# Weights staged through twelve slots and compared while they are copied; x, residual loads and y stores begun by GpSimd

## The reference

```
xn = layernorm(x)                                        # x: 16 x 512 x 512, float32
q, k, v = split(xn @ w_qkv.T + b_qkv)                    # 16 heads of 32
p = softmax(q @ k.T / sqrt(32) + causal)                 # per head 512 x 512
att = (p @ v) @ w_out.T + b_out
g = (xn @ gate.T) * gate_s;  u = (xn @ up.T) * up_s      # 1408 inner features, weights -1, 0, 1
ffn = ((silu(g) * u) @ down.T) * down_s
out = x + att + ffn
```

## Time and profile before

| | |
|---|---|
| Median of 3 runs | 2051.01 us (2050.69 to 2054.36) |
| Profiled execution, its own time | 2044.33 us |
| Its span, first to last instruction | 2041.0 us |
| Mean granted TensorE clock | 0.98 of full speed |
| Busy: PE, DVE, ACT, POOL | 1891.5, 1695.2, 1330.5, 1007.2 us |
| DMA: begun by SP's queue | 307.39 MB, 73.4% of 16 engines' span |

### The profile page before, as it was taken

How to read it: one execution, slowest core, us unless ns; L and a number is a source line. 1 busy time by engine, 2 the same in 40 slices (tenths; PEclk the granted TensorE clock), 3 DMA queues, 4 the chain that set the end, 5 groups by cost and what they waited for, 6 DMA issues and landing times.

```text
span 2041.0 us, 43778 instructions
## 1 busy us (share of the span) xinstructions
PE 1891.5 (93%) x14978; PEld 1225.1 (60%) x14978; DVE 1695.2 (83%) x5066; ACT 1330.5 (65%) x3723; POOL 1007.2 (49%) x1389
## 2 busy tenths in 40 slices
PE   5679999999999999999999999999999999989986
PEld 3447566665666656566665666656566665756663
DVE  3668888888888888888888898888888788888885
ACT  3747676665766667666666766666666666767673
POOL 5554554554554454554544545454554555454342
PEclk8889999999999999999999999999999999999998
DMA  6866867778677776868869787777877768676674
GB/s 196 222 125 128 185 133 163 153 136 177 134 165 146 149 162 136 179 133 163 153 135 181 139 163 150 145 175 129 180 136 161 142 137 175 130 171 122 132 147 94
DMA packets 832981, 310.24 MB, mean 152 GB/s; under 512 B 756464, under 2 KB 789232, under 8 KB 832752
## 3 DMA queue, kind: packets, MB, share of 16 engines
q1 hardware_dynamic: 832752, 307.39, 73.4%
HBM read 55.59 MB, written 16.78 MB: 35 GB/s over the span
## 4 chain that ended last, share of the span: by engine, by line
PE 39%; DVE 28%; SPq 14%; DMA 8%; ACT 6%; issue 4%; POOL 0%; DVEq 0%; ACTq 0%; POOLq 0%
PE bank L245 39%; SPq L819 10%; DVE phl L525 8%; DMA pt<-phl 7%; DVE bank L515 5%; ACT phl L428 4%; DVE fh L537 3%; DVE ft L533 2%; DVE small L506 2%; ACT bank L436 2%; DVE res L549 1%; SPq L826 1%; DVE small L487 1%; DVE xhl L660 1%; SPq L812 1%
## 5 line engine op out<-in xcount | busy, mean ns | idle before, releaser
L428 ACT ACTIVATE phl<-bank,small 128x512 f16<-128x512 f32 (+3 forms) x1024 | 500.2, 531 | 322.4 <-DVE small L506 217.7
L436 ACT ACTIVATE bank<-bank,small 128x512 f32<-128x512 f32 (+3 forms) x1024 | 514.4, 503 | 225.5 <-DVE small L515 218.6
L525 DVE SCALAR_TENSOR_TENSOR phl<-bank,small,phl 128x512 f16<-128x512 f32 (+3 forms) x1024 | 525.3, 544 | 102.1 <-ACT phl L428 98.3
L515 DVE CUSTOM_DVE_ANT_0 bank<-bank,mask 128x512 f32<-128x512 f32 (+3 forms) x1024 | 486.0, 505 | 109.3 <-PE bank L245 109.1
L718 POOL TENSOR_SCALAR ht<-fh 128x256 f16<-128x256 f32 x352 | 142.2, 404 | 602.1 <-DVE fh L537 602.1
L245 PE MATMUL bank<-xnT,wg 128*128 128x256 f16 x2816 | 368.0, 274 | 15.8 <-POOL wu L687 6.0
L245 PE MATMUL bank<-xnT,wu 128*128 128x256 f16 x2816 | 368.4, 274 | 0.0
L245 PE MATMUL bank<-xnT,wqkv 128*128 128x512 f16 x1536 | 355.9, 382 | 11.1 <-DMA xnT<-xhl 8.1
L245 PE MATMUL bank<-wd,ht 128*128 128x512 f16 x1408 | 330.4, 392 | 0.0
L245 PEld LDWEIGHTS bank<-xnT,wg 128*128 128x128 f16 x2816 | 262.2, 98 | 82.6 <-issue 13.2
L245 PEld LDWEIGHTS bank<-xnT,wu 128*128 128x128 f16 x2816 | 277.1, 98 | 33.5
(11 more groups left out here) (95 smaller groups left out, 1911.8 us busy)
## 6 DMA issues: line engine op xcount, KB each, us to landing
stk<-qkp SPq DMA_DIRECT2D x768, 64.0 KB, 2.1
res<-in_x_dram SPq DMA_DIRECT2D x64, 256.0 KB, 3.1
out_dram<-res SPq DMA_DIRECT2D x64, 256.0 KB, 2.4
xin<-in_x_dram SPq DMA_DIRECT2D x60, 256.0 KB, 3.2
pt<-phl SPq DMA_TRANSPOSE x512, 3.7
xin<-in_gate_dram SPq DMA_DIRECT2D x11, 256.0 KB, 3.3
xin<-in_up_dram SPq DMA_DIRECT2D x11, 256.0 KB, 3.3
xin<-in_down_dram SPq DMA_DIRECT2D x11, 256.0 KB, 3.4
```

The source lines that it names most:

```text
L428: i = eng.activation(phl[qt][:, j % 2, 0], pb[:, off:off + W], ACT.Copy, scale=st_r[:, c:c + 1])
L436: i = eng.activation(pb[:, off:off + W], pb[:, off:off + W], ACT.Exp, bias=st_m[:, c:c + 1], scale=-1.0, accum_out=st_s[:, c:c + 1])
L515: i = eng.tensor_tensor_reduce(out=bk[:, off:off + W], in0=bk[:, off:off + W], in1=mask[:, 512 - W:512], scale=-(32.0 ** -0.5) / (QS * QS) ...
L525: i = eng.scalar_tensor_tensor(phl[qt][:, j % 2, 1], pb[:, off:off + W], st_r[:, c:c + 1], phl[qt][:, j % 2, 0], ALU.mult, ALU.subtract)
```

## The change

Seven things change together.

- **Twelve staging slots**: four in the `res` tiles, four in `att`, four in `xnT[1]`. The first 24 chunks go through all twelve, the later ones through the first eight. The first 20 chunks are converted ahead of unit 0, then two per unit until unit 14; SP loads them two units ahead instead of three.
- **GpSimd converts all 33 plain chunks**, with a clamp to -1 and 1 in place of two multiplications by one. ScalarE converts none of them.
- **The check follows at once**: VectorE compares the staged float32 chunk with its 16-bit copy, one unit after the conversion (12 chunks ahead of unit 0, 21 in units 1 to 13), and a slot is free when that is done. The second loads and the reductions for the largest magnitude are gone; the clamp takes their place.
- **GpSimd begins the x loads, the residual loads and the y stores** (of the last batch SP still stores y), each with the wait that SP had.
- **Residual loads one unit later**: 12, 13, 15, 17 of the batch instead of 11, 12, 14, 16; the bias addition four units behind follows.
- **Layer norm of batch 1** at units 0, 4, 8, 12 like the others.
- **The stacking of q and k** goes by pairs of heads, with a semaphore each, so that the first five units of a group wait for the first pair only.

```diff
-            norm_at[12 + 2 * t if b == 1 else 40 * b - 40 + 4 * t] = (b, t)
-    check_at = {}
-    per = -(-3 * NI // (B - 5))
-    for i in range(3 * NI):
-        b, r = divmod(i, per)
-        check_at[40 * (b + 2) - 18 + 6 * r] = i
-    xin_order = sorted([(n, "norm", v) for n, v in norm_at.items()] + [(n, "check", v) for n, v in check_at.items()])
-    xin_use = {(kind, v): i for i, (n, kind, v) in enumerate(xin_order)}
-    xin_load_at = {n - 4: i for i, (n, kind, v) in enumerate(xin_order)}
-    nxs = {v: 4 + i for i, v in enumerate(v for n, kind, v in xin_order if kind == "norm")}
+            norm_at[40 * b - 40 + 4 * t] = (b, t)
+    xin_load_at = {n - 4: v for n, v in norm_at.items()}
     res_at = {}
     for b in range(B):
         for t in range(4):
-            res_at[15 + t if b == 0 else 40 * b + (11, 12, 14, 16)[t]] = (b, t)
+            res_at[15 + t if b == 0 else 40 * b + (12, 13, 15, 17)[t]] = (b, t)
...
-    stage = [xnT[1][:, 2 * i:2 * i + 2, :].rearrange("p a b -> p (a b)").bitcast(F32) for i in range(4)]
-    stage += [res[i][:, :] for i in range(4)]
+
+    stage = [res[i][:, :] for i in range(4)]
+    stage += [att[:, i // 2, 2 * (i % 2):2 * (i % 2) + 2, :].rearrange("p a b -> p (a b)").bitcast(F32) for i in range(4)]
+    stage += [xnT[1][:, 2 * i:2 * i + 2, :].rearrange("p a b -> p (a b)").bitcast(F32) for i in range(4)]
...
-        chunks.append(("plain", ("wg", i), gate[i], flat(wg[:, i]), None, "act"))
-        chunks.append(("plain", ("wu", i), up[i], flat(wu[:, i]), None, "pool"))
-        chunks.append(("plain", ("wd", i), down[i], wd[:, i], None, "act"))
+        chunks.append(("plain", ("wg", i), gate[i], flat(wg[:, i]), None, "check"))
+        chunks.append(("plain", ("wu", i), up[i], flat(wu[:, i]), None, "check"))
+        chunks.append(("plain", ("wd", i), down[i], wd[:, i], None, "check"))
...
-    W_FIRST = 17
...
+    W_FIRST, W_EARLY = 20, 18
...
+    slot_of = [n % 12 if n < 24 else n % 8 for n in range(NCH)]
+    turn_of = [slot_of[:n].count(slot_of[n]) for n in range(NCH)]
+    before = [max([m for m in range(n) if slot_of[m] == slot_of[n]], default=None) for n in range(NCH)]
+    slot_last = [max(n for n in range(NCH) if slot_of[n] == i) for i in range(12)]
...
+    finished = [(v_plain, plains[n]) if c[0] == "plain" else ready[c[1]] for n, c in enumerate(chunks)]
...
-            w.wait_ge(d_stk[G % 2], 192 * (G // 2 + 1))
+            w.wait_ge(d_stk[2 * (G % 2) + u // 5], 96 * (G // 2 + 1))
...
-            if kind == "plain" and last != "act":
+            if kind == "plain":
                 return
-            w.wait_ge(d_w[n % NST], 16 * (n // NST + 1))
-            eng.activation(hi, stage[n % NST], ACT.Copy, scale=WS if kind == "split" else 1.0).then_inc(a_w, 1)
+            w.wait_ge(d_w[slot_of[n]], 16 * (turn_of[n] + 1))
+            eng.activation(hi, stage[slot_of[n]], ACT.Copy, scale=WS).then_inc(a_w, 1)
...
-        drain_qk(0, 0)
-        drain_qk(0, 1)
-        for n in range(8, 11):
-            weight(n)
-        drain_qk(1, 0)
-        drain_qk(1, 1)
+        for G in range(2):
+            for c in range(2):
+                drain_qk(G, c)
         for f in range(F_FIRST):
-            for n in range(11 + 2 * f, 13 + 2 * f):
-                weight(n)
             tanh(f)
...
+        def check_plain(n):
+            kind, (name, k), src, w16, lo, last = chunks[n]
+            if kind == "plain":
+                i = ("wg", "wu", "wd").index(name) * NI + k
+                w.wait_ge(p_w, gp_count[n])
+                eng.scalar_tensor_tensor(stage[slot_of[n]], stage[slot_of[n]], 1.0, w16, ALU.mult, ALU.not_equal,
+                                         accum_out=miss[:, i:i + 1]).then_inc(v_plain, 1)
...
-        def check_plain(i):
-            kind, k = divmod(i, NI)
-            w16 = flat(wg[:, k]) if kind == 0 else flat(wu[:, k]) if kind == 1 else wd[:, k]
-            use = xin_use["check", i]
-            xi = xin[use % 2]
-            w.wait_ge(*ready[("wg", "wu", "wd")[kind], k])
-            w.wait_ge(d_xin[use % 2], 16 * (use // 2 + 1))
-            eng.scalar_tensor_tensor(xi[:, :], xi[:, :], 1.0, w16, ALU.mult, ALU.not_equal, accum_out=miss[:, i:i + 1]).then_inc(v_chk_plain, 1)
-            eng.tensor_reduce(large[:, i:i + 1], w16, AX.X, ALU.max, apply_absolute_value=True).then_inc(v_large, 1)
...
-            w.wait_ge(v_large, 3 * NI)
-            eng.tensor_scalar(large[:, :], large[:, :], 1.0, None, op0=ALU.is_gt).then_inc(v_end, 1)
+            w.wait_ge(v_plain, 3 * NI)
+            eng.tensor_reduce(flag_p[:, 0:1], miss[:, :], AX.X, ALU.add).then_inc(v_end, 1)
...
+        weight_low(0)
         first_low(2)
-        weight_low(0)
+        weight_low(1)
         first_low(3)
-        for n in range(1, 4):
-            weight_low(n)
+        weight_low(2)
+        weight_low(3)
+        for n in range(8, 11):
+            check_plain(n)
         v_low(0, 0, 0)
         for f in range(F_FIRST):
+            for n in range(11 + 3 * f, 14 + 3 * f):
+                check_plain(n)
             hidden(f)
...
-            if n in check_at:
-                check_plain(check_at[n])
+                scaled(4 * b + t, t, xs32[:, :], xin[t % 2][:, :])
+            for i in range(W_FIRST, NCH):
+                if w_slot(i) + 1 == n:
+                    check_plain(i)
...
-            sl = stage[n % NST]
-            if last != "pool":
-                return
+            sl = stage[slot_of[n]]
             if kind == "plain":
-                w.wait_ge(d_w[n % NST], 16 * (n // NST + 1))
-                eng.tensor_scalar(hi, sl, 1.0, 1.0, op0=ALU.mult, op1=ALU.mult).then_inc(p_w, 1)
-                return
-            splits = sum(c[0] == "split" and c[5] == "pool" for c in chunks[:n + 1])
-            w.wait_ge(a_w, act_count[n])
-            eng.tensor_scalar(sl, sl, WS, 1.0, op0=ALU.mult, op1=ALU.mult).then_inc(p_ws, 1)
-            w.wait_ge(p_ws, splits)
-            eng.tensor_tensor(lo, sl, hi, ALU.subtract).then_inc(p_w, 1)
+                w.wait_ge(d_w[slot_of[n]], 16 * (turn_of[n] + 1))
+                eng.tensor_scalar(hi, sl, 1.0, -1.0, op0=ALU.min, op1=ALU.max).then_inc(p_w, 1)
+            elif last == "pool":
+                w.wait_ge(a_w, highs[n])
+                eng.tensor_scalar(sl, sl, WS, 1.0, op0=ALU.mult, op1=ALU.mult).then_inc(p_ws, 1)
+                w.wait_ge(p_ws, lows["pool"][n])
+                eng.tensor_tensor(lo, sl, hi, ALU.subtract).then_inc(p_w, 1)
...
@@ -705,6 +694,9 @@
         def split_av(G):
             b, g = divmod(G, 4)
             w.wait_ge(s_o, 4 * b)
+            if G == 0:
+                for i in range(4, 8):
+                    w.wait_ge(*finished[slot_last[i]])
...
+
+        def load_x(b, t):
+            i = 4 * b + t
+            if i >= 6:
+                w.wait_ge(v_xs, i - 1)
+            eng.dma_start(xin[t % 2][:, :], x[b, 128 * t:128 * t + 128, :]).then_inc(d_xin[t % 2], 16)
+
+        def store_y(b, t):
+            w.wait_ge(v_oy, 4 * b + t + 1)
+            eng.dma_start(out[b, 128 * t:128 * t + 128, :], res[t][:, :]).then_inc(d_y[t], 16)
+
+        def load_res(b, t):
+            if b:
+                w.wait_ge(d_y[t], 16 * b)
+            else:
+                w.wait_ge(*finished[slot_last[t]])
+            eng.dma_start(res[t][:, :], x[b, 128 * t:128 * t + 128, :]).then_inc(d_res[t], 16)
...
-        weight(4)
-        weight(5)
+        for n in range(4, 11):
+            weight(n)
         split_qk(0, 0)
         split_qk(0, 1)
-        for n in range(6, 11):
+        for n in range(11, 14):
             weight(n)
         split_qk(1, 0)
         split_qk(1, 1)
...
         for f in range(F_FIRST):
-            for n in range(11 + 2 * f, 13 + 2 * f):
+            for n in range(14 + 2 * f, 16 + 2 * f):
                 weight(n)
             split_hidden(f)
-
+        load_x(1, 0)
...
-                w.wait_ge(d_xT[(i - 2) % 4], 16 * ((i - 2) // 4 + 1))
+                if t >= 2:
+                    w.wait_ge(d_xT[t - 2], 16 * (b + 1))
+                elif b >= 2:
+                    w.wait_ge(d_xT[t + 2], 16 * b)
+                else:
+                    w.wait_ge(d_xT[t], 16)
...
+            if n in xin_load_at:
+                load_x(*xin_load_at[n])
+            if n - 2 in o_at:
+                store_y(*o_at[n - 2])
+            if n in res_at:
+                load_res(*res_at[n])
...
         def load_weight(n):
-            if n >= NST:
-                w.wait_ge(*finished[n - NST])
-            eng.dma_start(stage[n % NST], chunks[n][2]).then_inc(d_w[n % NST], 16)
+            if before[n] is not None:
+                w.wait_ge(*finished[before[n]])
+            eng.dma_start(stage[slot_of[n]], chunks[n][2]).then_inc(d_w[slot_of[n]], 16)
...
-                for s in range(4):
-                    w.wait_ge(*finished[stage_last[s]])
+                for i in range(8, 12):
+                    w.wait_ge(*finished[slot_last[i]])
...
```

(52 more changed lines are left out.)

64 lines of the change are left out of this document (23 added, 41 removed).

## The result

The changed kernel takes 1988.18 us (median; 1984.16 to 1997.85), the kernel before, run beside it, 2052.69 (2050.69 to 2055.02): a ratio of 0.969 (0.965 to 0.973), 64.5 us less. The profiled execution took 1984.16 us, its span is 1982.3.

What follows compares the result with a forecast made beforehand. TensorE (PE) was taken as the bound in batches 1 to 14, held up by SP's issue time. Terms -65 (steady), -3, +8, -13 and -2 gave -75 us, from 2051.0 to 1976 us; range 1942 to 2032.

Steps and rivals of the forecast that it cites:

- SP as the holder of PE: Steady batches: SP's issue time, once a batch, delays transposes and holds up PE; the main reading, forecast chance 0.62.
- -35 (L525): Steady batches: of PE's 40.0 us waiting for the score bank, 35 us go (between 20 and 40).
- -15 ("issue"): Steady batches: PE's "issue" wait before the probability transpose lands shrinks, 15 us less over 14 batches (0 to 28).
- -12 (clock): Batches 1 to 14: the eight low-clock stretches behind the stall should go, 12 us less (0 to 14).
- the wait for L525 falls under 10: Sign that the forecast is right: PE's steady wait for the score bank falls from 40 to under 10 us.
- The checks in the steady batches: Eleven check batches: VectorE loses 57 us of comparisons and reductions beside PE's work; 3 us gained in all (0 to 12).
- Start: Before unit 0: conversions reordered, first mask addition at 46 to 47 us instead of 49.2; 3 us less.
- Batch 0, units 0 to 14: VectorE becomes the bound with 59 us of work, about 7 hidden in unit 14; 8 us more (0 to 20).
- Rest of batch 0: From unit 15 on: PE's 8.09 us wait at unit 23 goes, plus half of another 10; 13 less (8 to 18).
- The transfers, not SP: Rival, steady batches: transfer engines bind, so earlier-begun transposes land no earlier and stalls stay; about 2023 us, chance 0.16.
- VectorE at the start: Rival: comparisons slow to 1.5 us beside busier POOL, holding staging slots and SP; 15 us more, 1991 us, chance 0.12.
- POOL late: Rival, units 12 and 13: transfers above 1.3 us each delay x's high half; gain gone at 3.0 us; chance 0.10.

Runs made afterwards that it cites:

- e1: Kernel before, with y stores and residual loads begun by GpSimd in their old slots; 2010.8 us, ratio 0.981.
- e3: Changed kernel, with all x loads, residual loads and y stores begun by SP again; 2011.1 us, ratio 0.982.
- e12: Kernel before, second weight loads kept on SP, the check's comparisons and reductions left out; 2031.3 us, ratio 0.990.
- e5: Kernel before without the weights' check: second loads, comparisons and reductions left out; 2032.5 us, ratio 0.990.
- e6: Changed kernel with its comparisons left out, a slot being free once the 16-bit copy is written; 1963.7 us, ratio 0.957.
- e9: Changed kernel with reordered start, comparisons moved to batches 1 to 11 on second copies loaded by GpSimd; 1975.6 us, ratio 0.964.
- e4: Changed kernel with the first x load of batch 1 begun ahead of GpSimd's conversions; 1986.0 us, ratio 0.968.
- e8: Changed kernel, first x load ahead of conversions, V's low half ahead of three comparisons, two wqkv chunks converted earlier; 1977.0 us, ratio 0.964.
- e10: Changed kernel with twenty small writes on GpSimd ahead of every transfer it begins; 2006.3 us, ratio 0.979.
- e2: Kernel before with residual loads one slot later, all still begun by SP; 2034.6 us, ratio 0.993.
- e7: Changed kernel with residual loads back in their old slots (11, 12, 14, 16); 1994.2 us, ratio 0.972.
- e1b: Kernel before, y stores and residual loads begun by GpSimd, residual loads one slot later; 2016.7 us, ratio 0.985.

## Why the prediction was right, and where its terms were off

**The verdict.** Faster, and within the range; 12 us over the forecast of 1976. In the profile: -75 forecast, -58.7 measured.

**SP as the holder of PE: right, shown by e1 and e3.** Of -35 (L525), -15 ("issue") and -12 (clock) the profile shows -17.3, -25.8 and -13.6 (PE's work). The first lies below its lower bound of 20: I took a stall that goes for time that is saved, while 36 short waits for the same bank took its place. The second was undersized, the third near, though PE's work is not the clock alone: e1 loses as many low-clock stretches, seven, and only 8.1 us of work. But these rows hold more than the queue's part: alone, on the kernel before, it gives 37.5 us (e1), and from the changed kernel, x loads included, it takes 30.6 (e3), where the three terms were 62. The sign "the wait for L525 falls under 10" failed with the first term (22.7).

**The checks in the steady batches: -3 forecast, 12 to 17 measured (e12, e5).** The bound of 12 was there; I took its low end, since the work "lies beside PE's". It does, and its time shows all the same. That a comparison delays what stands behind it on VectorE, which feeds PE every unit, is my reading; no row follows one such delay to PE. The two errors nearly cancel, by luck: queue 37.5, check 12 to 17, together 50 to 55 of 58.6, and the remaining 4 to 9 are hardly more than single profiles tell.

**Start: -3 forecast, +0.8 measured.** The first mask addition came at 50.0. e6 and e9, with no comparison ahead of it, have it at 42.2 and 44.8, so the new order would have gained 4 to 7, and the twelve comparisons took that back.

**Batch 0, units 0 to 14: +8 forecast, +18.4 measured** (65.9 + 2.7 against 40.2 + 10.0). This step failed. VectorE is busy 54.2 us there, below my 59, so the work was sized well; it isn't full, because it stands 8.23 us in unit 0 before a load. "The number of x loads ... are as before" was true and missed that this load moves behind a long row of POOL's conversions; I looked at what stands behind a moved transfer, not at what stands ahead of it. That is part of the miss of 10.4: without this wait the units 0 to 14 take 62.7 us (e4), 5.9 less, and with the reordered start 60.8 (e8), still 10.6 over before. The comparisons are the larger cost: e6 keeps the wait (unit 0 takes 9.5 us) and has 46.3 for units 0 to 13. PE, idle 42% of these units, ran at a mean of 0.74 of its clock, where I had expected more clock than before. Hiding 7 us of unit 14 was right (10.0 to 2.7).

**Rest of batch 0: -13 forecast, -16.0 measured; end: -2 and -3.3 (within what single profiles tell).** PE's 8.09 us at unit 23 are gone, as forecast. The sum of the misses: 65 against 58.6 in the steady part, -8 against +3.2 up to batch 1.

**The rivals.** "The transfers, not SP" falls with e1: the transposes land no sooner after they are begun (3.8 us; 4.1 in the changed kernel, 3.7 before) and PE waits less. "VectorE at the start" named 1991, close to the result, but not by its sum: the 33 comparisons have a mean of 0.95 us, one alone took 1.64, and none of the others over 1.10. Two of their groups:

```profile
L486 DVE SCALAR_TENSOR_TENSOR res<-res,wu 128x512 f32<-128x512 f32 x6 | 5.5, 916 | 0.0
...
L486 DVE SCALAR_TENSOR_TENSOR att<-att,wu 128x512 f32<-128x512 f32 x3 | 3.2, 1083 | 1.6 <-POOL wu L676 1.6
```

Its other half did happen. In units 0 to 13 SP stood before weight loads whose slot a comparison had yet to free, 14.8 us of it in one piece, and behind that stood the first transpose of probabilities: it was begun 20.5 us after the first mask addition, 14.0 before. In e4 the piece is 8.2 us and the transpose comes after 14.8. SP's waits from 50 to 118 us, and its queue:

```profile
SPq L821 <- DVE res L486: 15.8, 4, 14.8
```

```profile
50.89 2.53 SPq L840 DMA_DIRECT2D stk<-qkp  x4
68.26 0.33 SPq L821 DMA_DIRECT2D res<-in_w_qkv_dram  x1
...
70.53 2.87 SPq L847 DMA_TRANSPOSE pt<-phl  x1
```

"POOL late" did not come because the price is low. The transfer as an operation of POOL (shortest, median and longest ns), and landings by group (page of the profile: KB each, median us to landing):

```profile
L737 POOL DMA_DIRECT2D out_dram<-res x60: 539/589/614, 223.6 to 1888.8; - x60
```

```profile
res<-in_x_dram POOLq DMA_DIRECT2D x64, 256.0 KB, 4.5
xin<-in_x_dram POOLq DMA_DIRECT2D x60, 256.0 KB, 4.6
out_dram<-res POOLq DMA_DIRECT2D x60, 256.0 KB, 3.6
```

I had taken 1.0 us and it is 0.59; the longest of the 184 took 0.76. The Trainium skill ("SBUF — State Buffer", "A bandwidth-pool intuition that's wrong") gives 3100 ns for one beside a VectorE copy; no transfer of this kernel shows that, with VectorE busy 87% of the time (1439 of 1652 us). Whether a price begins to tell at 1.3 us, and with 3 us a batch for each 1 us above, stays open, as e10's writes held up VectorE too. So does the turning point of 3.0 us, which no run comes near.

## What to carry to other kernels

When a queue that feeds the bounding engine stands full, find which of its entries nobody waits for soon, and have another engine begin them or begin them later; here either one alone helped, and after the first the second was worth nothing. An engine beside the bound is not free because it has idle time: a microsecond of VectorE's in the steady batches cost a quarter of itself (e12; a half in e9, with three more transfers a batch on POOL), and at the start, where VectorE is the busiest, some three quarters (e6: 24.5 us for 33 comparisons of 0.95 us). When an instruction moves to another queue, read what stands ahead of it at its first use too: one load behind a row of conversions left the busiest engine standing for 8 us, and 6 of them showed in the units behind (e4). And when an experiment adds work to one engine, look at the durations of the others before its time is read as a price (e10).

## What the runs showed of the hardware

- A 256 KB transfer begun by POOL costs it 0.59 us, much as SP's issue (0.43 to 0.58), but lands later: 4.5 us for the residual loads against 3.1 when SP begins them, 3.6 against 2.4 for the stores (medians). Why was not tried.
- Twenty one-column writes on POOL, 101 ns each in the profile, take 0.64 us together: to load an engine for a known time, sum the merged row of the timeline, not the mean of one. They also hold up VectorE: beside them L513 took 0.82 us and L522 behind it 1.13, against 0.17 and 0.56 beside a transfer that POOL begins.
- Low-clock stretches follow stalls of PE (the one that is left in the changed kernel, at 1546.9, follows a wait of 2.82 us that ends at 1546.50): 8, 9, 9 and 6 of them in batches 1 to 14 of the kernels whose PE is idle 60 to 72 us there, at most 3 where it is idle under 48, 6 in e3 (50.3); PE's work for the same matmuls spans 17 us (1640.3 in e2, 1623.0 in e7 and e8), but not in step with them: 1635.0 with three stretches (e1b), 1630.3 with six (e5).
